# A fused tokenizer, state-space and expert kernel: the router's small products are placed elsewhere, the gates get a buffer and a gather of their own, and the last state step is cut in two

## The reference

```python
h = concat([tokenizer(x), txt], axis=1)      # three patch levels in Hilbert order, two of them interpolated, one matmul
xz = layernorm(h) @ in_proj_w.T              # split in x and z; x: causal convolution of 4 taps, silu -> u
dt = softplus(u @ dt_w.T + dt_b); Bv = u @ B_w.T; Cv = u @ C_w.T
h_s = exp(dt * A) * h_s + dt * Bv * u        # scan over 384 tokens, 16 states for each channel
y = ((h_s * Cv).sum(states) + D * u) * silu(z)
h = h + layernorm(y @ out_w.T + residual) * ln_g + ln_b
xf = layernorm(h)
top2 of xf @ Wr.T -> gates by softmax of the two; 8 experts: gelu(xf @ Wi.T) @ Wo.T + bo
out = h + sum of gate * expert(xf) over the two experts
```

## Time and profile before

| | |
|---|---|
| median of 3 runs | 433.04 us (427.67 to 433.89) |
| the profiled execution | 433.38 us, of which the span is 431.6 |
| busy: PE, DVE, ACT, POOL | 379.8, 276.2, 200.5, 224.0 us |
| mean granted clock of TensorE | 0.941 of full speed |
| first stage; state steps | 0 to 77 us; 77 to 243 us |
| last rows and routing | 243 to 276 us |
| expert tiles; end | 276 to 418 us; to 431.6 |

### The profile page before, as it was taken

One profiled execution on the slowest core, in us unless ns is written; L12 is line 12 of the kernel. 1 busy time (PEld: TensorE's weight loads), 2 busy tenths in 40 slices (PEclk: granted clock), 3 DMA queues, 4 the chain that ended last, 5 costly groups with the idle time before them and its releaser, 6 DMA issues.

```text
span 431.6 us, 6906 instructions
## 1 busy us (share of the span) xinstructions
PE 379.8 (88%) x2285; PEld 286.8 (66%) x2285; DVE 276.2 (64%) x511; ACT 200.5 (46%) x516; POOL 224.0 (52%) x166
## 2 busy tenths in 40 slices
PE   5799989979996995779968898999999999999970
PEld 4465756646564662445634486799999999999970
DVE  4605456999899998997999596643444534434400
ACT  1347447674853546734547023144444354354440
POOL 6877730564636772756637200345565554655531
PEclk9969899999989996998979997799999999999995
DMA  6401103446574875497857544433333233232224
GB/s 168 78 6 11 7 3 70 122 120 137 116 147 122 232 243 165 158 270 210 294 167 189 150 209 74 113 83 59 49 46 61 43 49 56 44 52 48 39 28 118
DMA packets 37351, 46.98 MB, mean 109 GB/s; under 512 B 9485, under 2 KB 25950, under 8 KB 36750
## 3 DMA queue, kind: packets, MB, share of 16 engines
q1 hardware_dynamic: 29998, 38.94, 32.1%
q0 software_dynamic: 7328, 7.74, 12.2%
HBM read 40.65 MB, written 7.19 MB: 111 GB/s over the span
## 4 chain that ended last, share of the span: by engine, by line
PE 60%; DVE 17%; ACT 6%; DMA 5%; POOL 5%; issue 3%; SPq 1%; POOLq 0%; DVEq 0%; ACTq 0%
PE ps L1190 15%; PE ps L1171 10%; PE ps L1179 6%; DVE w_all L1760 5%; PE ps L1005 4%; DMA w_all<-bc_dram 3%; PE ps L1053 3%; PE ps L934 3%; POOL w_all L647 3%; POOL w_all L697 2%; DVE ps L1752 2%; PE ps L1007 2%; PE ps L1161 2%; DVE stats L1586 1%; DVE h_tok L1807 1%
## 5 line engine op out<-in xcount | busy, mean ns | idle before, releaser
L697 POOL TENSOR_TENSOR w_all<-w_all 128x768 f32<-128x768 f32 x47 | 78.9, 1682 | 82.4 <-DVE w_all L1760 36.6
L722 POOL DMA_INDIRECT sum_dram<-u_cm,tok_row x31 | 50.9, 1641 | 60.5 <-ACT u_cm L1551 53.8
L1005 PE MATMUL ps<-w_all,cst 128*128 128x512 f32 x96 | 55.4, 661 | 22.9 <-POOL w_all L697 22.3
L1760 DVE TENSOR_TENSOR_SCAN w_all<-decay,ps 128x780 f32<-128x780 f32 x40 | 71.1, 1779 | 2.0 <-POOL w_all L697 0.7
L706 POOL DMA_INDIRECT dt_cm<-x_dram,tok_in x31 | 30.8, 993 | 41.0 <-DVE texi L1989 29.0
L647 POOL DMA_INDIRECT w_all<-in_pix,gidx x42 | 44.1, 1051 | 14.9 <-issue 12.5
L1536 ACT ACTIVATE u_cm<-ps,x_cm 128x128 f32<-128x128 f32 x96 | 26.5, 376 | 39.8 <-PE ps L1179 39.8
L934 PE MATMUL ps<-cst 128*128 128x256 f32 x132 | 36.5, 433 | 5.5 <-DMA cst<-in_cst 4.9
L1005 PEld LDWEIGHTS ps<-w_all,cst 128*128 128x128 f32 x96 | 16.5, 198 | 35.4 <-POOL w_all L697 30.4
L1752 DVE TENSOR_TENSOR ps<-dtu_cm,ps 128x768 f32<-128x768 f32 x40 | 38.0, 949 | 2.7 <-ACT ps L1455 2.5
L1536 ACT ACTIVATE z_cm<-ps,y_cm 128x128 f32<-128x128 f32 x90 | 24.8, 375 | 27.5 <-PE ps L1179 27.5
(11 more groups left out here) (268 smaller groups left out, 706.8 us busy)
## 6 DMA issues: line engine op xcount, KB each, us to landing
w_all<-bc_dram SPq DMA_DIRECT2D x48, 256.0 KB, 3.6
w_all<-bc_dram SPq DMA_DIRECT2D x96, 64.0 KB, 3.8
w_all<-in_w_all SPq DMA_DIRECT2D x20, 289.0 KB, 4.5
w_all<-in_w_all SPq DMA_DIRECT2D x3, 1156.0 KB, 8.9
b_wide_sb<-bc_dram SPq DMA_DIRECT2D x8, 256.0 KB, 3.9
x_dram<-x_cm SPq DMA_DIRECT2D x3, 384.0 KB, 4.6
sum_dram<-h_tok SPq DMA_DIRECT2D x3, 384.0 KB, 4.3
out<-sum_dram SPq DMA_DIRECT2D x4, 288.0 KB, 3.7
```

The source lines that it names most:

```text
L697: nc.gpsimd.tensor_tensor(segments(hcs[at % 2]), inner(states[at % 2]), segments(c_sb[at % RING]), ALU.mult).then_inc(hc_rdy, 1)
L722: pool.indirect_dma_start(sum_dram, bass.IndirectOffsetOnAxis(ap=tok_row[:, i:i + 1].bitcast(U32), axis=0), y_out[:, i % 2, :], None, comp ...
L1005: nc.tensor.matmul(sums[:, 0:4 * P], ident, hcs[at % 2][:, 0:4 * P], start=False, stop=at % S == S - 1, skip_group_check=True)
L1760: v.tensor_tensor_scan(states[p], fade, drive, 0.0, ALU.mult, ALU.add).then_inc(scanned, 1)
```

## The change

- **First stage.** PE's `router_weights` goes from before `coarse_levels` to after `coarse_rows` (its banks are 1 and 0 now), two warm matmuls stand in its old place, and `first_rows` goes from before `interpolated` to after `fused_tokens(0)`, with two warm matmuls inside it. DVE's `router_weights` goes behind `softplus(0)`, ACT's two copies behind `squares_of`. The warm count "normed rows" is 4 instead of 7, "slots" 18 for 20, "first tile" 3 for 4.
- **Weights.** The buffers of the first stage are put in another order in `w_all`. SP loads seven pieces in the first stage, five at steps 7 to 15, and eight from step 16 on, one in three steps.
- **Inserted work.** The top two are found at `s == 8`, `new_h` is at `s == 9`, `row_shift` at 11, ACT's second deviation at 10 and `router_rows` at 13; POOL's waits move with them.
- **Rows and gates.** `send_rows(0)` is at step 34 and `send_rows(1)` after the loop. Each stores the rows twice, to `x_first` (256 columns) and to `x_dram`. The gates live in `gate_x` and go to `gate_dram` and to `x_dram` in pieces of two floats. POOL's first four gathers read `x_first`, four further small gathers read `gate_dram`, the later ones read `x_dram`.
- **Last step and routing.** The last product, the last sum, and `chunk_output(2)` are each cut into four segments and two. `hot`, `pos`, `pos_k` have the tokens innermost. The gates are computed after the one-hot tables; these are made in four parts; the 24 slot matmuls write their columns twice (`r=2`); `found` is gone.
- **Bias rows** go to banks 4 to 7 instead of 0 to 5, those of chunk 2 after the first `up`.
- **Output.** ACT issues two of the four output DMAs.

```diff
-        WARM = {... "normed rows": 7, ... "slots": 20, "bias rows": 1, "first tile": 4}
+        WARM = {... "normed rows": 4, ... "slots": 18, "bias rows": 1, "first tile": 3}
             def send_rows(j):
                 sp.wait_ge(xf_rdy, j + 1)
-                sp.dma_start(x_rows(j, 0, C), xf[:, NB * j:NB * j + NB, 0:C]).then_inc(x_sent, 16)
+                for dst, signal in ((x_first, x_sent), (x_dram, rows_sent)):
+                    sp.dma_start(rows_of(dst, j, slice(0, C)), xf[:, NB * j:NB * j + NB, 0:C]).then_inc(signal, 16)
+                    sp.dma_start(rows_of(dst, j, slice(C, CW)), xf[:, NB * j:NB * j + NB, P:C]).then_inc(signal, 16)
             def send_gates(j):
-                sp.dma_start(x_rows(j, C, XW), xf[:, NB * j:NB * j + NB, P:XF]).then_inc(x_sent, 16)
+                for dst, columns in ((gate_dram, slice(0, TOPK)), (x_dram, slice(CW, XW))):
+                    sp.dma_start(rows_of(dst, j, columns), gate_x[:, NB * j:NB * j + NB, :]).then_inc(gates_sent, 16)
             store_bc(0)
+            sp.wait_ge(coarse_ps, 4)
+            sp.wait_ge(rearr, 2)
+            for piece in loads[0:7]:
+                load_expert(*piece, PIECES)
...
-                if at > S and at % S == 14:
-                    send_rows(at // S - 1)
+                if at == 2 * S + 2:
+                    send_rows(0)
...
-                if at >= S and at % 4 != 3 and loaded < len(loads):
+                if (7 <= at < S and at % 2 == 1 or at >= S and at % 3 == 1) and loaded < len(loads):
...
             for i in range(NX):
-                fetch(i)
+                fetch(i, x_first, slice(0, CW), xin_l[i])
+            pool.wait_ge(gates_sent, 16 * 2 * NJ)
+            for i in range(NX):
+                fetch(i, gate_dram, slice(CW, XW), gate_l[i])
+            pool.wait_ge(rows_sent, 16 * 2 * NJ)
...
             z_projection(0, 6)
             coarse_transposes()
-            router_weights()
+            keep_warm(WARM["coarse levels"], 4)
             coarse_levels()
...
             keep_warm(WARM["fine patches"], 0)
-            first_rows()
+            router_weights()
             interpolated(0)
...
             fused_tokens(0)
+            first_rows()
             keep_warm(WARM["normed rows"], 0)
...
+            def last_sum():
+                pe.wait_ge(last_hc, 1)
+                nc.tensor.matmul(sums[:, 0:4 * P], ident, hcs[(STEPS - 1) % 2][:, 0:4 * P], ...).then_inc(last_low, 1)
+                pe.wait_ge(last_hc, 2)
+                nc.tensor.matmul(sums[:, 4 * P:6 * P], ident, hcs[(STEPS - 1) % 2][:, 4 * P:6 * P], ...).then_inc(summed, 1)
...
-                                          what[:, 0:2 + k, :, t], start=(t == NT), stop=(t == NT - 1),
+                                              at_lo[:, :, t], what[:, 0:w, :, t].rearrange("p (o w) m -> p o w m", o=1)
+                                              .to_broadcast([P, 2, w, MT]), start=(t == NT), stop=(t == NT - 1),
...
             x_transposed(0, 0)
-            pe.wait_ge(h_final, NB)
             up(0, 0)
-            pe.wait_ge(h_final, NB + 2)
+            last_bias_rows()
...
                     if s == 8:
                         deviation(1 + 2 * n)
-                    elif s == 9:
+                    elif s == 10:
                         deviation(2 + 2 * n)
-                    elif s == 12:
+                    elif s == 13:
                         router_rows(n - 1)
...
+            act.wait_ge(y_sent, 16 * MT)
+            for b in range(2, NB):
+                act.dma_start(out[b], sum_dram[L * b:L * b + L, :]).then_inc(out_st, 16)
...
             dve.wait_ge(x_sent, 16 * 2 * NJ)
+            dve.wait_ge(rows_sent, 16 * 2 * NJ)
             first_e = up_weights(0, 0)
-            for b in range(NB):
...
+            bias_rows(0)
+            bias_rows(1)
             tokens(0, 0)
-            gates(0, 0)
+            bias_rows(2)
+            bias_rows(3)
             def expert_tile(i, q):
...
+                        down_weights(0, 0, first_e)
+                        dve.wait_ge(bo_ps, 2 * NB)
+                        for h in range(2):
+                            v.tensor_tensor(h_tok[:, 2, 2 * h:2 * h + 2, :], h_tok[:, 2, 2 * h:2 * h + 2, :],
+                                            ps[:, 6:8, 256 * h:256 * h + C], ALU.add).then_inc(h_final, 1)
+                        gates(0, 0)
+                        down_weights(1, 1, e)
+                        gates(1, 1)
```

270 lines of the change are left out of this document (150 added, 120 removed).

## The result

The changed kernel took 442.74 us (median of 4 runs, 439.39 to 447.43), the kernel before 431.85 us beside it (4 runs, 427.67 to 433.89): a ratio of 1.0235, 95% interval 1.0127 to 1.0344. A second set on another chip gave 442.12 against 433.26 us, 1.0195 (1.0125 to 1.0265). So it is slower, by 1.3 to 3.4% in the first set, where 425.7 us had been forecast. Medians here are of all executions of a run, ratios and intervals of those in the chip's faster state alone. The profiled execution took 445.11 us with a span of 443.3, against 433.38 and 431.6.

The account below looks back on a forecast made before the run. Bounds: a PE, ACT, PE, DVE chain first, DVE in state steps, a DVE, PE, DVE, store, gather chain, then PE in expert tiles. +0.1 - 1.9 + 0.3 - 5.7 - 0.5 = -7.7 from 433.38: 425.7 us, range 421 to 431.5.

Parts of the forecast that it names:

- the term 5.46: First stage: PE's first_rows, two warm matmuls and four more behind fused_tokens take 5.46 us together.
- the cover is used up: First stage: PE's list ends at 56.28, normed rows were taken up at 56.12; +0.1 remains of the -1.33 us.
- if those waits were gone: First stage: DVE's router_weights and ACT's copies lie in waits; without those they would cost about 1.1 and 0.5 us.
- Gain in front of it: First stage: coarse_levels 0.63 us earlier, first_rows giving its place to router_weights 0.70; fused_tokens 1.33 earlier.
- 0, and about 1 if that slack is gone: State steps: send_rows(0)'s four DMAs ahead of C for step 35, taken up some 5 us after them, cost 0.
- hide behind DVE's longer steps: State steps: POOL's waits for the top two and for new_h, in the inserted work, stay hidden.
- The ACT table reload at step 28: State steps: ACT reloads its table right before the decay of step 29; +0.3 us, between 0 and 1.3.
- doubled columns cost 0: Slot matmuls: twice the columns cost 0 while weight loads set the pace; at half clock at most +0.3 us.
- rival D: Gate stores land late, DVE waits in gates(0), up_weights(2) is queued behind; at 4 us each 439.4 us, chance 0.07.
- rival B: Half clock as up(0) starts, half of 4 us lost: +2.2, 427.9 us, chance 0.20.
- Rival E: Second pair of row stores: rows_sent lands at 270, not 265.7, delaying DVE's first weight copy; +4.3, 430 us, chance 0.12.
- POOL's queue makes that up over the tiles: Expert tiles: sum_dram gets its rows 1.5 us after the first y is ready; the tiles recover that.

Follow-up runs that it names:

- f13: e8 without gate_dram: gates stored once, beside their rows in x_dram, and the first four tiles fetch them from there; 424.99 us, 0.986 of the kernel before.
- f15: f13 with the change's order of the first stage; 431.51 us, 0.9983 of the kernel before.
- f16: f15 without the six warm matmuls behind fused_tokens; 426.23 us, 0.9878 of the kernel before.
- e4: Changed kernel with one copy of the rows (x_first) and one of the gates (gate_dram); 478.96 us against 469.9 for the kernel before, 1.0249.
- e8: Changed kernel with old first-stage order, single slot columns, late second row copy and x_dram gates, POOL's row_shift wait, output on SP; 431.32 us, 0.9938 of the kernel before.
- e5: Changed kernel with the 24 slot matmuls writing their columns once instead of twice; 435.91 us against 433.26 for the kernel before, 1.0035.
- f14: Changed kernel, all six gate stores kept, gate_dram's pairs 256 bytes apart; 438.12 us against 431.99 for the kernel before, 1.0178.

## Why the prediction was wrong, step by step

Four terms of the sum failed: PE's list in the first stage (priced 5.46 us, took 9.3), the row stores ahead of a broadcast (0, took 2.5), the doubled columns of the slot matmuls (0, took 3.2), and the gate stores in front of the first gather (0, took 2.5 to 3.3). The wait of `row_shift` for POOL (1.5) was not in the sum at all.

**First stage: the term 5.46 was sized at the wrong clock.** The list was counted right, item by item, and it took 9.3 us instead of 5.46, because every item was priced from rows at full clock. The cover it was laid against had no slack (by the forecast itself the list ended at 56.28, behind 56.12), so all of the excess was path. The sentence "the cover is used up" should have led to a range of several us to one side. f13, f15 and f16 confirm the place and give the order's price, 6.5 us. The condition beside it, that DVE's `router_weights` would cost about 1.1 "if those waits were gone", came true in five later profiles, at 1.16 to 2.48 us.

**Gain in front of it: lost as well.** `coarse_levels` started 0.28 us earlier instead of 0.63, but ran its 32 small matmuls in 2.08 us instead of 3.59 and had `coarse_rows` done 3.4 us earlier. `fused_tokens` kept 0.9 of that, less than the 1.33 forecast: the clock fell next and `interpolated` took 2.93.

**`send_rows(0)`: "0, and about 1 if that slack is gone" failed.** Slack was taken from the time between issue and use, 5 us, and the time that four stores of rows take ahead of the broadcast was left out. e4 and e8, which store one copy there, have no late C. The wait at step 37 was 2.5 us in the profiled execution and 1.8 to 2.9 in the seven others that keep both copies at step 34. The gain on step 36 was there (-1.76 against -1.9), and so was the last product's (-1.09 against -1.05).

**POOL's waits: "hide behind DVE's longer steps" was true of the waits and missed the rest.** Taking POOL's wait for `row_shift` away let POOL start its multiplication 0.02 us before it, and DVE paid 1.52 us. The ACT table reload at step 28 was charged +0.3 and cost nothing: between scans 16 and 32 lie 50.9 us in both kernels.

On this the Trainium skill (SBUF — State Buffer, SBUF: two separate sides) says that a DVE instruction with two SBUF inputs and a GpSimd instruction that reads SBUF exclude each other: whichever starts first holds the shared port pair for its whole length, and the other is blocked. The trace agrees: POOL's starts 0.02 us ahead and lasts 1.69 us, DVE's lasts 1.68, and 0.16 without POOL beside it.

**Slot matmuls: "doubled columns cost 0" was wrong.** The row's 3.60 us over 24 is 0.15, and a weight load lasts 0.148, so the loads seemed to set the pace "for 93 columns". But the 0.15 is a mean of two forms, twelve matmuls of 93 columns 0.17 us apart and twelve of 62 only 0.115 apart. The row names the first form alone; a closer look at the same trace would have shown that the pace follows the columns, and that doubling them costs about twice 3.60. The 3.2 us measured (e5 takes 3.0 of them away again) are the largest part of this stretch that an edit shows.

The Trainium skill (SBUF — State Buffer, its note on SBUF "cachelines") says that each access which crosses to a new 16-byte line pays a penalty. Here each column of `what` lies 48 bytes from the last and costs 1.8 ns. The matmuls that spread B, also bfloat16 but with neighbouring columns, start 0.11 us apart for 256 columns, 0.4 ns each, in the kernel before:

```profile
188.35 0.27 PE L983 MATMUL ps<-b_parts,pick 128*128 128x256 bf16 x1
188.46 0.22 PE L984 MATMUL ps<-b_parts,pick 128*128 128x128 bf16 x1
```

The trace agrees as far as that goes; no run changed the stride alone.

**Gate stores: the resource of rival D, and not its path.** From the first gather to `up(0)` pass 8.7 us where 5.4 were forecast (263.7 to 269.1). Rival D (chance 0.07) had the stores slow, but laid their cost on DVE's wait in `gates(0)`. That wait did not come: DVE got there at 289.98 and went on. I had looked only at who waits for the gates; the gather of rows, issued behind the stores, was slowed by them and paid first. And the price was read from runs of 264 bytes by counting runs, where the distance of their targets counts too (f14). With stores as fast as f14's or f13's PE waits for no rows any more, and in f13 `up(0)` starts 5.4 us behind the first gather, as forecast. Rival E did not happen: in front of DVE's first copy of weights (276.98) stands no wait for rows.

**Half clock at `up(0)`: rival B came true beside D**, 2.93 and 1.42 us (L1223) against 1.58 and 0.94 (L1179), 1.8 us. I had treated the rivals as alternatives; they add up.

**What was right.** POOL's gather directly behind `tok_in`; the slot matmuls' start, 19.25 us behind the last product instead of 21.76 (forecast 258.5 - 239.85 = 18.65); no DMA wait at the last product. With single columns and the gates' addresses apart, f13's first `down` came 35.5 us behind the last product, where the forecast of all its terms was 40.43 - 4.65 = 35.8. Output: forecast -0.5 (0 to -1.2), measured nothing: f13, with all stores on SP, needs 7.0 us, the split 7.04. That is the end of the range without a gain.

The sum: forecast -7.7, span +11.7. The 19.4 between them are 5.0 (first stage), 4.1 (steps), 8.25 (last product to first `down`: about 3.2 columns, 2.5 to 3.3 landing, 1.8 clock) and 2.0 behind it, of which 0.5 is the output's missing gain. Of the other 1.5, 0.8 lie in the tiles (135.58 us from first to last `down`, before 134.76), most of it in one tile where PE waits for a gather from `x_dram`:

```profile
317.26 0.44 PE L1205 MATMUL ps<-cst,dt_cm 128*128 128x128 f32 x2 [0.49 <-DMA dt_cm<-x_dram,tok_in]
```

"POOL's queue makes that up over the tiles" was thus nearly right: the first scatter waits 3.68 us for `h_tok` in `sum_dram` and comes 4.65 us behind its `down` instead of 2.96, and f13, with the same lateness, loses nothing by it. The last 0.7, a last scatter 0.3 later and output stores 0.4 longer, is not explained.

## What to carry to other kernels

A filler or a small product laid against a cover with no slack must be priced at both clocks: here the list went from 5.46 to 9.3 us, and what it was laid against (DVE's normed rows) did not slow down with it. When a duration can be set by two things that cost the same, look first whether the row is a mean of several forms, which may tell them apart; if not, double one of them on the chip, or keep the double price in the range. In this kernel small stores to DRAM had to be judged by the distance of their targets as well as by their number: written beside the rows they belong to, they let the gather behind them through. Ask first which gather is issued behind them, and how soon.
